# A decoder layer on one core: the scaling of the key rows moved to GpSimd, the second value copy of each row to ScalarE

## Chip, cores and metric

One core of a Trainium2 chip runs the whole kernel in one launch. The metric is the device time of one execution in microseconds, the median of several runs. Engines: TensorE (PE; PEld are its weight loads), VectorE (DVE), ScalarE (ACT), GpSimd (POOL), SyncE (SP), which issues the DMAs. Each engine works through its own program in order and waits for the others by semaphores.

## What is computed

```python
x = layernorm(x + attn(x))            # x: (2, 256, 512); 32 heads of 16, ALiBi, causal
x = layernorm(x + cross(x, ctx))      # ctx: (2, 512, 512); 32 query heads, 8 key/value heads of 128
x = layernorm(x + ffn(x))             # 16 groups of 32 -> 128 -> 32, gelu

# cross attention, the part that the change touches:
kv = concatenate([ctx, x], axis=1)    # 768 rows for each of the 2 samples, 1536 in all
k = (kv @ Wk).reshape(..., 8, 128)
v = (kv @ Wv).reshape(..., 8, 128)
k = k * rsqrt(mean(k * k, -1) + 1e-6) * k_norm_w
```

Products are kept exact to float32 by splitting each operand into a high and a low part and making three passes (hi x hi, hi x lo, lo x hi).

## The kernel before

There are three stages: self-attention with the keys and values of cross-attention (function `self_attention_and_keys`), cross-attention, feed-forward. The change lies in the first.

**Self-attention** goes by 16 quads of four heads. For quad c, TensorE makes the scores S(c) (L699). Then for each of four heads i: VectorE adds the ALiBi bias and takes the row's extreme (E, `softmax_shift`, L514); ScalarE takes the exponential and its sum (E, L398); VectorE takes reciprocals of two heads' sums at a time (R, L523); GpSimd multiplies by them (R, `normalise`, L349 and L351) and makes the bias for the next quad (`alibi`, L344); TensorE transposes (T(c,i), L709); VectorE copies the result out of PSUM (L529). Each second quad TensorE weighs the values (PV, L721), and ScalarE (A, L405) and VectorE (A, L535) split the result into high and low.

**Key and value rows** are 12 rows n of 128 tokens, eight of ctx and four of x after the first layernorm. The work of a row on TensorE is cut into eight parts (n,0) to (n,7), two for each group of 512 columns: parts 0 and 1 make the first half of the keys (g = 0), 2 and 3 the second (g = 1), 4 and 5 the first half of the values, 6 and 7 the second. A part is six 128x512 matmuls. `g_ps` counts finished groups. What follows a group:
- keys, g: ScalarE copies PSUM to `k_rows` (L422, at part 2 or 4) and squares it (L427); VectorE sums (L554) and makes the mean plus epsilon (`k_ms`, L557, at part 3 or 5); GpSimd raises to -1/2 (`k_inv`, L377, same part); VectorE multiplies `k_rows` in place by `k_inv`, broadcast over 128 columns (L564, at part 5 for g = 0 and 7 for g = 1); TensorE transposes in the next row's parts 1 and 3 (KT(n,g), L738); ScalarE copies to `kT_st` with the norm weights (L412).
- values: VectorE copies PSUM to `v_st` (`take_values`, L543), the first half at part (n,6), the second at part (n+1,0).
- SyncE stores `v_st` when `vg_out` has counted both halves (L307), and `kT_st` when `kt_out` has (L309), and before the next stage's first load waits for all stores.

x rows come late: Y and LN (L606 to L612), the power for the layernorm on GpSimd (L380), X1 (L620), transposes XT (L794), and their split by ScalarE (L483) and VectorE (L615).

**Order.** `order_of_work` (L81 to L150) writes out one list for all engines; each engine runs the entries that concern it, in that order. Row parts stand between the steps of the quads, so that TensorE has matmuls while the other engines do the softmax. An excerpt, from quad 13 on: `S14, (8,0), E(14,0), T(13,0), KT(7,0), (8,1), E(14,1), T(13,1), (8,2), E(14,2), T(13,2), KT(7,1), (8,3), E(14,3), R(14,0), T(13,3), R(14,1), S15, PV6, (8,4), E(15,0), A6, T(14,0), (8,5), E(15,1), T(14,1)`. Around row 6: `E(10,2), T(9,2), (6,0), XT1, E(10,3), R(10,0), T(9,3), KT(5,0)`. Around quad 4: `(2,3), W7, R(4,1), S5, PV1`, where W7 is four 128x512 subtractions on GpSimd (L336).

**PSUM.** Transposes and PV share banks 4 and 7 in turn (RING), the row groups share 5 and 6 (GROUPS). Before it writes a bank TensorE waits until the last user has been drained (`drained`, L633 to L653): after a T for VectorE's copy, after a PV for VectorE's low half, after a KT for ScalarE, after a second x1 transpose for VectorE's low half, after a value group for `vg_out`.

Of the kernel before, what the change touches and what calls it, by code (L numbers as in the profile page):

```python
# [12 lines left out]
P = 128  # L13
ALU = mybir.AluOpType
ACT = mybir.ActivationFunctionType
# [137 lines left out]
def self_attention_and_keys(nc, d, k):  # L153

    with ExitStack() as ctx:
# [68 lines left out]
        kinv_made, knrm_made = t.sem("kinv_made"), t.sem("knrm_made")  # L224
        vg_out = t.sem("vg_out")
        kt_ps, kt_out = t.sem("kt_ps"), t.sem("kt_out")
# [41 lines left out]
        def _(sp):  # L268
# [31 lines left out]
            for n in range(ROWS):  # L300
                if n + 2 < B * CT:
                    load_context(n + 2)
                if n == 1:
                    load_weights(7)
                if n == 4:
                    load_weights(8)
                sp.wait_ge(vg_out, 2 * n + 2)  # L307
                sp.dma_start(v_view[:, :, rows_of(n), :], v_st[:]).then_inc(v_store, 16)
                sp.wait_ge(kt_out, 2 * n + 2)  # L309
                sp.dma_start(k_view[:, :, rows_of(n), :], kT_st[:]).then_inc(k_store, 16)  # L310
# [6 lines left out]
        def _(pool):  # L317
# [44 lines left out]
            for what, a in ORDER:  # L362
# [8 lines left out]
                elif what == "part":  # L371
                    n, r = a
                    if r in (3, 5) and n < ROWS:
                        g = r // 2 - 1
                        w = slice(GH * g, GH * (g + 1))
                        pool.wait_ge(kms_made, 2 * n + g + 1)
                        nc.gpsimd.tensor_tensor(k_inv[:, w], k_ms[:, w], minus_half[:, w], ALU.pow).then_inc(kinv_made, 1)  # L377
                elif what == "LN":
                    pool.wait_ge(var_made, a + 1)
                    nc.gpsimd.tensor_tensor(rstd[:, a:a + 1], var[:, a:a + 1], minus_half[:, 0:1], ALU.pow)\  # L380
                        .then_inc(rstd_made, 1)

        @block.scalar
        def _(act):
# [29 lines left out]

            def part(n, r):
                if r in (2, 4) and n < ROWS:
                    g = r // 2 - 1
# [73 lines left out]
        def _(dve):  # L491
# [46 lines left out]

            def take_values(n, g):
                dve.wait_ge(g_ps, 4 * n + g + 3)  # L540
                if n >= 1:
                    dve.wait_ge(v_store, 16 * n)
                nc.vector.tensor_copy(v_st[:, GH * g:GH * (g + 1), :].rearrange("p h e -> p (h e)"),  # L543
                                      bank[:, bank_of("part", (n, 4 + 2 * g)), :]).then_inc(vg_out, 1)

            def part(n, r):
                if r == 0 and n >= 1:
                    take_values(n - 1, 1)
                if n == ROWS:
# [8 lines left out]
                if r == 6:  # L558
                    take_values(n, 0)
                if r in (5, 7):  # L560
                    g = r // 2 - 2
                    w = slice(GH * g, GH * (g + 1))
                    dve.wait_ge(kinv_made, 2 * n + g + 1)
                    nc.vector.tensor_tensor(k_rows[:, w, :], k_rows[:, w, :], k_inv[:, w].rearrange("p (h a) -> p h a", a=1)  # L564
                                            .to_broadcast([P, GH, HD]), ALU.mult).then_inc(knrm_made, 1)

# [65 lines left out]
        def _(pe):  # L632
            def drained(what, a):  # L633
# [12 lines left out]
                elif held == "XT":  # L646
                    pe.wait_ge(x1t_lo, i + 1)
                elif held == "Y":
                    pe.wait_ge(y_sum, i + 1)
                elif i[1] < 4:  # L650
                    pe.wait_ge(kg_out, 2 * i[0] + i[1] // 2 + 1)
                else:
                    pe.wait_ge(vg_out, 2 * i[0] + i[1] // 2 - 1)  # L653

# [1056 lines left out]
```

## Time and profile before

| | us |
|---|---|
| median of 3 runs | 885.67 (884.92 to 885.82) |
| profiled execution | 883.53 |
| its span | 881.7 |
| TensorE busy | 834.4 (95%) |
| VectorE busy | 567.6 (64%) |
| GpSimd busy | 505.6 (57%) |
| ScalarE busy | 462.6 (52%) |

The first stage takes about the first 283 us of the span. In rows of groups the columns are: line, engine, operation, output<-input, shapes, count; then busy time in us and mean ns of one; then the engine's idle time before them and who ended it. In rows of the timeline: start and duration in us, engine, line, operation, and in brackets the engine's idle time before it and who ended that. Consecutive instructions of one engine overlap by some 0.1 us.

### The profile page before, as it was taken

What the parts mean: (1) busy time and instruction counts of PE and PEld (TensorE: products, weight loads), DVE (VectorE), ACT (ScalarE), POOL (GpSimd) and SP (SyncE); (2) the same over time, 40 slices, a digit from 0 to 9 for tenths busy, and PEclk for the clock granted to TensorE, in tenths of its full rate; (3) what the DMA queues carried; (4) which work ended last, traced back from release to release, by engine and by line L of the source; (5) the groups of instructions that cost most, each with busy time, mean ns of one, the idle gap of its engine ahead of it and who ended that gap; (6) DMA issues with size and microseconds to landing.
All of it is one profiled execution on the core that took longest, in us unless ns stands there. A gap on an engine that the chain in (4) does not pass through costs nothing. (4 is left out here: it accounts for less than half of the span.)

```text
span 881.7 us, 15131 instructions
## 1 busy us (share of the span) xinstructions
PE 834.4 (95%) x4833; PEld 698.2 (79%) x4833; DVE 567.6 (64%) x1538; ACT 462.6 (52%) x981; POOL 505.6 (57%) x655
## 2 busy tenths in 40 slices
PE   7999999899898699999999999999999999999975
PEld 5777776677676688888888888888888888888753
DVE  4377675777542576676677667667667767777535
ACT  5666653555322365555556456555555645556242
POOL 2565863665311786756765775775675676445711
PEclk9999999999999699999999999999999999999978
DMA  6503132121113621121121122122121102000011
GB/s 223 183 26 132 63 100 81 56 64 49 48 48 96 222 67 66 36 67 67 37 65 65 36 65 65 36 65 65 36 65 65 36 12 67 1 1 1 0 25 48
DMA packets 48463, 56.23 MB, mean 64 GB/s; under 512 B 4622, under 2 KB 29724, under 8 KB 48412
## 3 DMA queue, kind: packets, MB, share of 16 engines
q1 hardware_dynamic: 48412, 55.59, 20.0%
q8 instruction: 27, 0.44, 0.2%
q14 instruction: 24, 0.20, 0.1%
HBM read 41.95 MB, written 13.63 MB: 63 GB/s over the span
## 5 line engine op out<-in xcount | busy, mean ns | idle before, releaser
L1090 POOL TENSOR_SCALAR prob<-prob,x_rinv 128x768 f32<-128x768 f32 x128 | 116.2, 908 | 166.8 <-DVE x_rinv L1265 166.8
L1207 ACT ACTIVATE pT_hi<-bank 128x512 fp32r<-128x512 f32 x192 | 114.4, 597 | 96.6 <-PE bank L1422 96.0
L1186 ACT ACTIVATE prob<-bank,x_nm,q_rms 128x768 f32<-128x768 f32 x128 | 127.1, 993 | 49.2 <-DVE x_nm L1259 48.9
L1256 DVE TENSOR_REDUCE x_mx<-bank 128x1 f32<-128x768 f32 x128 | 122.1, 954 | 26.3 <-PE bank L1380 26.2
L1318 DVE TENSOR_TENSOR pT_lo<-bank,pT_hi 128x512 fp32r<-128x512 f32 x192 | 130.4, 680 | 8.5 <-ACT pT_hi L1207 6.9
L1422 PE MATMUL bank<-ident,prob 128*128 128x128 f32 x768 | 116.2, 274 | 5.3 <-POOL prob L1090 5.3
L1422 PEld LDWEIGHTS bank<-ident,prob 128*128 128x128 f32 x768 | 95.8, 141 | 17.6 <-POOL prob L1090 6.4
L398 ACT ACTIVATE s_self<-s_self,nm_self 128x128 f32<-128x128 f32 (+1 forms) x128 | 57.0, 447 | 66.5 <-DVE nm_self L514 66.4
L48 PE MATMUL bank<-pT_hi,xv_hi 128*128 128x512 f32 x192 | 86.6, 451 | 0.9 <-DVE pT_lo L1318 0.8
L50 PE MATMUL bank<-pT_hi,xv_lo 128*128 128x512 f32 x192 | 75.8, 395 | 0.0
L49 PE MATMUL bank<-pT_lo,xv_hi 128*128 128x512 f32 x192 | 75.4, 393 | 0.0
L1380 PE MATMUL bank<-xk_hi,qT_hi 128*128 128x384 f32 x256 | 69.3, 352 | 2.5 <-DVE xk_lo L1284 2.4
L1380 PE MATMUL bank<-xk_lo,qT_hi 128*128 128x384 f32 x256 | 67.2, 344 | 0.0
L1380 PE MATMUL bank<-xk_hi,qT_lo 128*128 128x384 f32 x256 | 67.1, 343 | 0.0
L48 PE MATMUL bank<-w_hi,cT_hi 128*128 128x512 f32 x128 | 56.3, 440 | 1.2 <-DVE x_rows L606 1.2
L377 POOL TENSOR_TENSOR k_inv<-k_ms,minus_half 128x4 f32<-128x4 f32 x24 | 27.7, 1155 | 50.3 <-DVE k_ms L557 49.8
L1216 ACT ACTIVATE oT_hi<-bank 128x512 fp32r<-128x512 f32 x32 | 19.1, 598 | 70.3 <-PE bank L50 70.3
L1380 PEld LDWEIGHTS bank<-xk_hi,qT_hi 128*128 128x128 f32 x256 | 46.7, 193 | 11.3 <-issue 2.8
L48 PE MATMUL bank<-wo_hi,oT_hi 128*128 128x512 f32 x128 | 52.2, 408 | 0.0
L48 PE MATMUL bank<-wq_hi,x_hi 128*128 128x512 f32 x128 | 51.9, 406 | 0.0
L49 PE MATMUL bank<-w_lo,cT_hi 128*128 128x512 f32 x128 | 50.6, 395 | 0.0
L50 PE MATMUL bank<-w_hi,cT_lo 128*128 128x512 f32 x128 | 50.5, 395 | 0.0
(196 smaller groups left out, 2042.8 us busy)
## 6 DMA issues: line engine op xcount, KB each, us to landing
wo_raw<-in_Wo SPq DMA_DIRECT2D x8, 1024.0 KB, 5.4
wq_raw<-in_Wq SPq DMA_DIRECT2D x7, 1024.0 KB, 5.5
v_by_head<-v_st SPq DMA_DIRECT2D x12, 512.0 KB, 3.3
kT_by_head<-kT_st SPq DMA_DIRECT2D x12, 512.0 KB, 3.2
xk_raw<-kT_by_head SPq DMA_DIRECT2D x16, 384.0 KB, 3.2
xv_raw<-v_by_head SPq DMA_DIRECT2D x16, 384.0 KB, 3.1
wq_raw<-in_w_attn SPq DMA_DIRECT2D x12, 256.0 KB, 4.4
xk_raw<-in_ctx SPq DMA_DIRECT2D x8, 256.0 KB, 2.5
```

Source lines behind the costliest of these rows:

```text
L48: nc.tensor.matmul(out, a_hi, b_hi, start=first, stop=False)
L49: nc.tensor.matmul(out, a_hi, b_lo, start=False, stop=False)
L50: return nc.tensor.matmul(out, a_lo, b_hi, start=False, stop=last)
L377: nc.gpsimd.tensor_tensor(k_inv[:, w], k_ms[:, w], minus_half[:, w], ALU.pow).then_inc(kinv_made, 1)
L398: nc.scalar.activation(s_sb[:, c % 2, i, a:e], s_sb[:, c % 2, i, a:e], ACT.Exp, bias=nm[:, c % 2, i, qt:qt + 1], scale=-1.0, accum_out=rsu ...
L1090: nc.gpsimd.tensor_scalar(prob[:, s, :], prob[:, s, :], rinv[:, s:s + 1], 1.0, ALU.mult, ALU.mult)\
L1186: nc.scalar.activation(prob[:, s, :].rearrange("p (a e) -> p a e", a=2), bank[:, at:at + 2, 0:HALF], ACT.Exp, bias=nm[:, s:s + 1], scale=q ...
L1207: nc.scalar.activation(pT_hi[:, a, :], bank[:, turn.bank[s, what, a], :], ACT.Copy)\
L1256: nc.vector.reduce_max(mx[:, s:s + 1], bank[:, at:at + 2, 0:HALF], AX.XY)\
L1318: nc.vector.tensor_tensor(pT_lo[:, a, :], bank[:, turn.bank[s, what, a], :], f32(pT_hi[:, a, :]), ALU.subtract).then_inc(ring_out, 1)
L1380: last = nc.tensor.matmul(bank[:, at + c, 0:HALF], a_hi[:, g, w], k_part[:, b, c * HALF:(c + 1) * HALF], start=start, stop=stop)
L1422: last = nc.tensor.transpose(bank[:, at, j * P:(j + 1) * P], prob[:, UT * (s % 2) + j, a * P:(a + 1) * P], ident[:])
```

## The change

The product of `k_rows` and `k_inv` is issued by GpSimd, right behind the power of the same g at parts 3 and 5 and behind a wait for that power, where VectorE issued it at parts 5 and 7. The copy of the second value half, at part (n+1,0), is issued by ScalarE, at the head of that part, and counts on a semaphore of its own, `vg_late`; the first half stays on VectorE. SyncE and TensorE wait for the two semaphores accordingly.

```diff
--- before.py
+++ after.py
@@ -222,7 +222,7 @@
         g_ps = t.sem("group_ps")
         kg_out, ksq_made, kss_made, kms_made = t.sem("kg_out"), t.sem("ksq_made"), t.sem("kss_made"), t.sem("kms_made")
         kinv_made, knrm_made = t.sem("kinv_made"), t.sem("knrm_made")
-        vg_out = t.sem("vg_out")
+        vg_out, vg_late = t.sem("vg_out"), t.sem("vg_late")
         kt_ps, kt_out = t.sem("kt_ps"), t.sem("kt_out")
         q_ps, q_rows_out, ss_part = t.sem("q_ps_cross"), t.sem("q_rows_out"), t.sem("ss_part1")
         k_store, v_store = t.sem("k_store"), t.sem("v_store")
@@ -304,7 +304,8 @@
                     load_weights(7)
                 if n == 4:
                     load_weights(8)
-                sp.wait_ge(vg_out, 2 * n + 2)
+                sp.wait_ge(vg_out, n + 1)
+                sp.wait_ge(vg_late, n + 1)
                 sp.dma_start(v_view[:, :, rows_of(n), :], v_st[:]).then_inc(v_store, 16)
                 sp.wait_ge(kt_out, 2 * n + 2)
                 sp.dma_start(k_view[:, :, rows_of(n), :], kT_st[:]).then_inc(k_store, 16)
@@ -375,6 +376,9 @@
                         w = slice(GH * g, GH * (g + 1))
                         pool.wait_ge(kms_made, 2 * n + g + 1)
                         nc.gpsimd.tensor_tensor(k_inv[:, w], k_ms[:, w], minus_half[:, w], ALU.pow).then_inc(kinv_made, 1)
+                        pool.wait_ge(kinv_made, 2 * n + g + 1)
+                        nc.gpsimd.tensor_tensor(k_rows[:, w, :], k_rows[:, w, :], k_inv[:, w].rearrange("p (h a) -> p h a", a=1)
+                                                .to_broadcast([P, GH, HD]), ALU.mult).then_inc(knrm_made, 1)
                 elif what == "LN":
                     pool.wait_ge(var_made, a + 1)
                     nc.gpsimd.tensor_tensor(rstd[:, a:a + 1], var[:, a:a + 1], minus_half[:, 0:1], ALU.pow)\
@@ -413,6 +417,12 @@
                                      bank[:, bank_of("KT", (n, g)), :], ACT.Copy, scale=nw[:]).then_inc(kt_out, 1)
 
             def part(n, r):
+                if r == 0 and n >= 1:
+                    act.wait_ge(g_ps, 4 * n)
+                    if n >= 2:
+                        act.wait_ge(v_store, 16 * (n - 1))
+                    nc.scalar.activation(v_st[:, GH:KVH, :].rearrange("p h e -> p (h e)"),
+                                         bank[:, bank_of("part", (n - 1, 6)), :], ACT.Copy).then_inc(vg_late, 1)
                 if r in (2, 4) and n < ROWS:
                     g = r // 2 - 1
                     w = slice(GH * g, GH * (g + 1))
@@ -536,16 +546,14 @@
                                                scalar=cols[:, 2 * KT + m:2 * KT + m + 1], in1=f32(xT_hi[:, m, w]),
                                                op0=ALU.add, op1=ALU.subtract).then_inc(at_lo, 1)
 
-            def take_values(n, g):
-                dve.wait_ge(g_ps, 4 * n + g + 3)
+            def take_values(n):
+                dve.wait_ge(g_ps, 4 * n + 3)
                 if n >= 1:
                     dve.wait_ge(v_store, 16 * n)
-                nc.vector.tensor_copy(v_st[:, GH * g:GH * (g + 1), :].rearrange("p h e -> p (h e)"),
-                                      bank[:, bank_of("part", (n, 4 + 2 * g)), :]).then_inc(vg_out, 1)
+                nc.vector.tensor_copy(v_st[:, 0:GH, :].rearrange("p h e -> p (h e)"),
+                                      bank[:, bank_of("part", (n, 4)), :]).then_inc(vg_out, 1)
 
             def part(n, r):
-                if r == 0 and n >= 1:
-                    take_values(n - 1, 1)
                 if n == ROWS:
                     return
                 if r in (3, 5):
@@ -556,13 +564,7 @@
                     dve.wait_ge(kss_made, 2 * n + g + 1)
                     nc.vector.tensor_scalar(k_ms[:, w], k_ss[:, w], 1.0 / HD, RMS_EPS, ALU.mult, ALU.add).then_inc(kms_made, 1)
                 if r == 6:
-                    take_values(n, 0)
-                if r in (5, 7):
-                    g = r // 2 - 2
-                    w = slice(GH * g, GH * (g + 1))
-                    dve.wait_ge(kinv_made, 2 * n + g + 1)
-                    nc.vector.tensor_tensor(k_rows[:, w, :], k_rows[:, w, :], k_inv[:, w].rearrange("p (h a) -> p h a", a=1)
-                                            .to_broadcast([P, GH, HD]), ALU.mult).then_inc(knrm_made, 1)
+                    take_values(n)
 
             for j in range(TT):
                 dve.wait_ge(xt_hi, j + 1)
@@ -649,8 +651,10 @@
                     pe.wait_ge(y_sum, i + 1)
                 elif i[1] < 4:
                     pe.wait_ge(kg_out, 2 * i[0] + i[1] // 2 + 1)
+                elif i[1] == 4:
+                    pe.wait_ge(vg_out, i[0] + 1)
                 else:
-                    pe.wait_ge(vg_out, 2 * i[0] + i[1] // 2 - 1)
+                    pe.wait_ge(vg_late, i[0] + 1)
 
             pe.wait_ge(const, 4)
             for j in range(TT):
```

## Rows read from the trace of the kernel before

**Rows 1.** Windows view, the changed stage: stretch, then busy us of each engine.
```profile
45.00:283.00 238.00, 225.44 (x1508) 174.07 (x1506) 149.16 (x508) 118.95 (x356) 117.39 (x222) 1.00 0.22 68
```

**Rows 2.** Table of waits in the stage: waiter, releaser, total us, times, longest.
```profile
PE bank L709 <- DVE pT_self L529: 3.3, 3, 2.0
```

**Rows 3.** Groups in the stage: busy us, mean ns, idle before and releaser.
```profile
L564 DVE TENSOR_TENSOR k_rows<-k_rows,k_inv 128x512 f32<-128x512 f32 x24 | 16.9, 706 | 0.9 <-POOL k_inv L377 0.9
...
L377 POOL TENSOR_TENSOR k_inv<-k_ms,minus_half 128x4 f32<-128x4 f32 x24 | 27.7, 1155 | 50.3 <-DVE k_ms L557 49.8
...
L543 DVE COPY v_st<-bank 128x512 f32<-128x512 f32 x24 | 16.3, 679 | 1.3 <-PE bank L50 1.2
...
L422 ACT ACTIVATE k_rows<-bank 128x512 f32<-128x512 f32 x24 | 14.0, 582 | 3.0 <-PE bank L50 3.0
...
L361 POOL TENSOR_TENSOR x_rows<-x_rows,pT_self 128x512 f32<-128x512 f32 x4 | 5.1, 1304 | 0.0
```

**Rows 4.** Timeline, VectorE and GpSimd side by side: start, us, engine, line.
```profile
77.91 0.17 DVE L557 TENSOR_SCALAR k_ms<-k_ss 128x4 f32<-128x4 f32 x1
...
77.99 0.69 DVE L564 TENSOR_TENSOR k_rows<-k_rows,k_inv 128x512 f32<-128x512 f32 x1
...
78.16 1.38 POOL L377 TENSOR_TENSOR k_inv<-k_ms,minus_half 128x4 f32<-128x4 f32 x1 [3.01 <-DVE k_ms L557]
...
96.16 0.86 DVE L557 TENSOR_SCALAR k_ms<-k_ss 128x4 f32<-128x4 f32 x1
```

**Rows 5.** Timeline around KT(0,0).
```profile
64.53 0.69 DVE L564 TENSOR_TENSOR k_rows<-k_rows,k_inv 128x512 f32<-128x512 f32 x1 [0.38 <-POOL k_inv L377]
...
66.39 0.63 PE L738 MATMUL bank<-ident,k_rows 128*128 128x128 f32 x4 [0.71 <-DVE pT_self L529]
```

**Rows 6.** Timeline at S(14).
```profile
201.30 0.94 PE L699 MATMUL bank<-kT_even,qT 32*128 32x128 f32 x16 [0.61 <-DVE nm_self L514]
```

**Rows 7.** Timeline, T(15,0) and T(15,1), and the value copy between.
```profile
222.10 0.55 PE L709 MATMUL bank<-ident,s_self 128*128 128x128 f32 x3 [1.09 <-POOL s_self L351]
...
225.21 0.68 DVE L543 COPY v_st<-bank 128x512 f32<-128x512 f32 x1
...
226.50 0.52 PE L709 MATMUL bank<-ident,s_self 128*128 128x128 f32 x3 [2.02 <-DVE pT_self L529]
```

**Rows 8.** Timeline before T(9,2).
```profile
157.68 0.89 DVE L564 TENSOR_TENSOR k_rows<-k_rows,k_inv 128x512 f32<-128x512 f32 x1
...
162.59 0.52 PE L709 MATMUL bank<-ident,s_self 128*128 128x128 f32 x3 [0.92 <-DVE pT_self L529]
```

**Rows 9.** Timeline, GpSimd's normalisation of quad 4 and T(4,2).
```profile
96.98 0.88 POOL L349 TENSOR_SCALAR s_self<-s_self,rinv_self 128x128 f32<-128x128 f32 x1
...
97.84 0.47 POOL L351 TENSOR_SCALAR s_self<-s_self,rinv_self 128x256 f32<-128x256 f32 x1
...
98.83 0.49 PE L709 MATMUL bank<-ident,s_self 128*128 128x128 f32 x3
```

**Rows 10.** Timeline, second x1 transpose's ScalarE half and KT(5,0).
```profile
165.80 0.58 ACT L483 ACTIVATE x_hi<-bank 128x512 fp32r<-128x512 f32 x1
...
167.24 0.63 PE L738 MATMUL bank<-ident,k_rows 128*128 128x128 f32 x4 [1.30 <-DVE x_lo L615]
```

**Rows 11.** Timeline from the power of row 8 to T(14,1).
```profile
209.52 1.01 POOL L377 TENSOR_TENSOR k_inv<-k_ms,minus_half 128x4 f32<-128x4 f32 x1 [3.11 <-DVE k_ms L557]
...
212.78 0.29 DVE L514 CUSTOM_DVE_ANT_0 s_self<-bank,alibi 128x128 f32<-128x128 f32 x1 [1.46 <-POOL alibi L344]
...
214.90 0.48 DVE L535 SCALAR_TENSOR_TENSOR x_lo<-bank,cols,x_hi 128x256 fp32r<-128x256 f32 x1 [1.48 <-ACT x_hi L405]
...
215.67 0.49 PE L709 MATMUL bank<-ident,s_self 128*128 128x128 f32 x3
```

**Rows 12.** Timeline, normalisation of quad 1 and T(1,0).
```profile
58.04 0.48 POOL L351 TENSOR_SCALAR s_self<-s_self,rinv_self 128x256 f32<-128x256 f32 x1
...
59.99 0.49 PE L709 MATMUL bank<-ident,s_self 128*128 128x128 f32 x3
```

## Prediction

> **What bounds the kernel.** I read five views, in this order. First the page: TensorE is busy for most of the span, so only its idle time can shrink. Then the windows view of the changed stage, from the first key row's work to the last key transposes [rows 1]: TensorE is busy 225.44 of 238.00 us, so 12.6 us is all that any relief of another engine can give. VectorE is busy 149.16, ScalarE 118.95 and GpSimd 117.39 us there: none is full, and what counts is when each answers. The table of waits [rows 2] says who was late: mostly VectorE. The groups give prices [rows 3]; the timeline gives each stall its place. TensorE has 14 stalls there; below are the ones that the change can touch. The rest have nothing removed or added just ahead of them, and I leave them.
>
> **What is removed.** VectorE loses 24 products of 706 ns and 12 value copies of 679 ns [rows 3]: 16.9 + 8.1 = 25.1 us. That is no gain by itself; it counts where TensorE stands waiting for VectorE with a removed instruction shortly before.
> - KT(0,0), 0.71 us [rows 5]: it waits for a bank that VectorE drains, and VectorE had first waited 0.38 us for the inverse norm and then scaled for 0.69. Both go: all 0.7 is regained.
> - S(14), 0.61 us [rows 6]: it waits for the last shift of quad 13. Ahead of that stand, in VectorE's order, both products of row 7, some 0.6 us each with the overlap. Gain 0.6, all that TensorE waits.
> - T(15,1), 2.02 us [rows 7]: it waits for the copy of T(15,0), which VectorE makes after a value copy that started at 225.21. That copy leaves: some 0.6, less 0.1 for what comes late upstream (below), so 0.5. The four weight subtractions before it remain.
> - T(9,2), 0.92 us [rows 8]: a product of 0.89 us at 157.68 is in the chain, but the next shift also needs a bias from GpSimd, which will be later. Between 0 and 0.9; I take 0.3, near the low end, as the bias follows closely.
>
> Sum of gains: 0.7 + 0.6 + 0.5 + 0.3 = 2.1 us.
>
> **What GpSimd pays.** 24 products at 128x512. The trace has no broadcast operand on GpSimd; the nearest row is the in-place addition of the same size, 1304 ns [rows 3]. The low end is VectorE's own 706 ns; the high end is 1.30 plus one VectorE product waited out, 0.69: 2.0 us. I take 1.30, the same engine, size and kind. The handoff from the power to the product through GpSimd's own semaphore is not shown; across engines it took 0.08 us (78.08 to 78.16 [rows 4]), and I take that: 1.38 us per product, 33 us in all, behind each of the 24 powers (1155 ns). Some comes back: a power took 1.38 us while VectorE's product ran beside it, against 1.01 alone [rows 4, 11], and 0.88 us went into a 128x128 normalisation beside one [rows 9]. That is 0.4 to 0.5 us for each collision, and these products leave.
>
> The rows put the product at 1304 ns on GpSimd against 706 on VectorE [rows 3]. The Trainium skill speaks against such a move (GPSIMD Engine Reference, Elementwise — side-by-side cycle accounting): a two-input operation costs GpSimd about twice VectorE's time, 4497 ns at 2048 elements. By proportion, an estimate from that page is 1.12 us for 512, by which the sum below would be 0.2 us better, the cost at T(4,2) halved.
>
> Queued behind the product are normalisations and biases, and behind these TensorE's transposes and VectorE's shifts. Site by site:
> - T(1,0): its normalisation ended at 58.52 and TensorE came at 59.99 [rows 12]: slack 1.47 against 1.38. No cost, narrowly. T(9,0) stands the same way.
> - T(4,2): normalisation over at 98.31, TensorE at 98.83 [rows 9]: slack 0.52. The shift is 1.38 less the 0.5 of the collision that leaves, 0.88. Cost 0.35.
> - T(14,1): a power at 209.52 stands before the normalisation and the bias that VectorE waited 1.46 us for; then come shift, exponential, ScalarE's and VectorE's halves of the attention output, whose end (215.38) frees the bank that T(14,1) takes at 215.67 [rows 11]. 1.38 - 0.29 = 1.1 us late. But T(15,0) stalls 1.09 us for another reason [rows 7], VectorE having two products in between; without them VectorE has caught up to within 0.1. So this cost is swallowed by that stall: nothing, apart from the 0.1 above, and T(15,0) gives nothing.
> - Elsewhere GpSimd was idle before its next work for longer than 1.4 us, or the collision returned the difference. There the product costs nothing; if that cover went, each would cost up to 1.4.
> - The reverse collision: k_ms took 0.86 us beside a GpSimd subtraction [rows 4]. The product starts after k_ms and a power, when VectorE mostly reads PSUM; nothing, at most 0.7 once or twice.
>
> **What ScalarE pays.** 12 copies at 582 ns [rows 3], 7.0 us. It waits for the group that VectorE waited for, at the same place in its order, and queued behind are exponentials, key evictions and the x1 halves. In most rows ScalarE is waiting for the next shift then: nothing, and 0.6 each if it weren't. One place is bare: in row 6 the copy stands between an exponential and the second x1 half, which already ran back to back at 165.80, and TensorE waited 1.30 us for its other half [rows 10]. Cost 0.6.
>
> **Queues.** The value store gets two waits for one and is issued when the later copy is done, 0.1 us sooner. The end of the stage is set by the last key store, behind the last key transposes, for which the last product comes a whole group of TensorE work early. No DMA is added, and GpSimd's queue has none. The two later stages are untouched.
>
> **Sum.** -2.1 + 0.35 + 0.6 = -1.15 us. The profiled execution took 883.53 us (span 881.7 and 1.8 around it), so I expect 882.4 with a span of 880.5. The median of the runs is 885.67, 2.1 above the profiled one; carried over: 884.5 us. What a measurement of this kernel can tell from no change is about 0.2%, 1.8 us.
>
> **Rivals.**
> (a) GpSimd becomes the late engine. The place is the normalisation behind a power; it decides from a product of 1.39 us, where the 1.47 of T(1,0) is used up with the handoff. At 2.0 us (2.08 with handoff): T(1,0) and T(9,0) 0.6 each, T(4,2) 1.1, T(14,1) 1.8 of which 1.1 is swallowed, 0.7, and ScalarE's 0.6: 3.6 us. The gains at KT(0,0), T(9,2) and T(15,1) go, since each needs GpSimd's next bias or normalisation early; 0.6 is left at S(14): +3.0, so 888.7. For it: slacks that equal the price to 0.1 us; against: all additions and subtractions of this size lie near 1.3. Chance 0.18, all sizes of it.
> (b) All of VectorE's stalls close: 0.71 + 0.92 + 0.61 + 2.02 and GpSimd's 1.09 at T(15,0) [rows 5 to 8] are 5.35 us, so 880.3 at the most; half of it, 883.0, is the likelier form. For it: VectorE is the releaser of nearly all. Against: behind several stands ScalarE's half or a weight subtraction, which stay. Chance 0.17.
> (c) Nothing moves: what VectorE gives up was hidden, and later joints between the engines re-form each stall. 885.7. For it: VectorE is only 63% busy in the stage (149.16 of 238). Chance 0.15.
> The forecast, small gains against smaller losses, has 0.50.
>
> **How the numbers follow.** The forecast case spreads by about 1 us either way, as it is a difference of five small terms: a fifth of it lies beyond 1.8 us faster, hardly any beyond 1.8 slower. With most of (b), faster by over 0.2% gets 0.25; with most of (a), slower gets 0.16; the rest, 0.59, is within. The range takes in half of (b), all of (c) and (a) up to a product of about 1.7 us: 882.4 to 887.6.
>
> **What would show it.** Right: the GpSimd product at 1.2 to 1.4 us; powers uniformly near 1.02; the stalls at KT(0,0) and S(14) gone, that of T(15,1) near 1.5, T(15,0)'s below 0.3; new stalls at T(4,2) (0.3) and T(14,1) (1.0); the one at KT(5,0) grown to 1.9. TensorE's idle time in the stage near 11.4. Wrong: a product above 1.45 us with new GpSimd stalls at T(1,0) and T(9,0), or fewer than 10 us idle, or a changed start of the next stage's transposes apart from the shift.

## The result, and the profile after

The kernel after takes **879.52 us** (median of 7 runs, 879.4 to 881.52) against 884.92 (7 runs of the kernel before beside it, 882.54 to 886.67): ratio 0.9948, 95% interval 0.9932 to 0.9963. That is 4.6 us faster by the ratio, four times the forecast of 1.15, and outside the range of 882.4 to 887.6 on the fast side. Its span is 877.6 us against 881.7.

The windows view of the changed stage, as in [rows 1], once over the same stretch and once cut where the stage now ends: TensorE's first transposes of the next stage (L1369, after L1373) moved from 287.63 to 284.24, 3.39 us, and 283.00 - 3.39 = 279.61.

```profile
45.00:283.00 238.00, 225.10 (x1509) 174.13 (x1507) 128.43 (x472) 126.25 (x368) 136.57 (x246) 1.00 0.23 71
...
45.00:279.61 234.61, 225.10 (x1509) 174.13 (x1507) 128.43 (x472) 125.71 (x368) 136.57 (x246) 1.00 0.22 69
```

TensorE's idle time in the stage is 234.61 - 225.10 = 9.5 us, where it was 12.6 and the forecast had 11.4. VectorE lost 20.7 us there, GpSimd gained 19.2, ScalarE 6.8.

Who TensorE waited for (table of waits, 45 to 283: waiter, releaser, total, times, longest), to be held against [rows 2] and [rows 5 to 10]:

```profile
PE bank L742 <- DVE x_lo L617: 1.8, 1, 1.8
PE bank L713 <- POOL s_self L350: 1.4, 1, 1.4
...
PE bank L713 <- DVE pT_self L539: 0.9, 2, 0.5
PE bank L713 <- DVE x_lo L545: 0.8, 1, 0.8
...
PE bank L713 <- POOL s_self L352: 0.2, 1, 0.2
```

The largest is KT(5,0), grown as foreseen; the 1.4 is T(15,1), shrunk; the 0.9 are T(9,2) and T(9,3); 0.8 is the new T(14,1), 0.2 the new T(4,2). KT(0,0), S(14), T(15,0) and a stall that the prediction had not listed, KT(4,0), are gone. The groups of after in the same stretch, the counterparts of [rows 3]:

```profile
L352 POOL TENSOR_SCALAR s_self<-s_self,rinv_self 128x256 f32<-128x256 f32 x64 | 31.5, 493 | 0.0
L350 POOL TENSOR_SCALAR s_self<-s_self,rinv_self 128x128 f32<-128x128 f32 x64 | 25.1, 392 | 19.5 <-DVE rinv_self L533 18.8
L380 POOL TENSOR_TENSOR k_rows<-k_rows,k_inv 128x512 f32<-128x512 f32 x24 | 25.0, 1040 | 1.9
L378 POOL TENSOR_TENSOR k_inv<-k_ms,minus_half 128x4 f32<-128x4 f32 x24 | 24.6, 1023 | 43.2 <-DVE k_ms L565 42.8
...
L553 DVE COPY v_st<-bank 128x512 f32<-128x512 f32 x12 | 8.2, 681 | 0.6 <-PE bank L50 0.6
L424 ACT ACTIVATE v_st<-bank 128x512 f32<-128x512 f32 x12 | 7.0, 583 | 6.6 <-PE bank L50 6.5
```

The product on GpSimd takes **1040 ns**, not 1304; the power fell from 1155 to 1023 (23 of the 24 lie at 1.01 to 1.03 us, one at 1.24). The timeline of after at the places of the steps: quad 1's normalisation behind a power and its product and T(1,0) [rows 12], KT(0,0) without a wait, T(4,2), the ScalarE copy ahead of the second x1 half, KT(5,0), T(14,1), T(15,1):

```profile
56.71 1.03 POOL L378 TENSOR_TENSOR k_inv<-k_ms,minus_half 128x4 f32<-128x4 f32 x1 [2.09 <-DVE k_ms L565]
57.82 1.04 POOL L380 TENSOR_TENSOR k_rows<-k_rows,k_inv 128x512 f32<-128x512 f32 x1
58.84 0.37 POOL L350 TENSOR_SCALAR s_self<-s_self,rinv_self 128x128 f32<-128x128 f32 x1
59.20 0.48 POOL L352 TENSOR_SCALAR s_self<-s_self,rinv_self 128x256 f32<-128x256 f32 x1
...
60.03 0.49 PE L713 MATMUL bank<-ident,s_self 128*128 128x128 f32 x3
...
65.58 0.60 PE L742 MATMUL bank<-ident,k_rows 128*128 128x128 f32 x4
...
97.98 0.55 PE L713 MATMUL bank<-ident,s_self 128*128 128x128 f32 x3 [0.23 <-POOL s_self L352]
...
163.25 0.57 ACT L424 ACTIVATE v_st<-bank 128x512 f32<-128x512 f32 x1
163.72 0.58 ACT L493 ACTIVATE x_hi<-bank 128x512 fp32r<-128x512 f32 x1
...
165.18 0.63 PE L742 MATMUL bank<-ident,k_rows 128*128 128x128 f32 x4 [1.78 <-DVE x_lo L617]
...
213.90 0.52 PE L713 MATMUL bank<-ident,s_self 128*128 128x128 f32 x3 [0.82 <-DVE x_lo L545]
...
223.12 0.52 PE L713 MATMUL bank<-ident,s_self 128*128 128x128 f32 x3 [1.41 <-POOL s_self L350]
```

At T(1,0) the handoff from power to product through GpSimd's own semaphore cost 57.82 - 57.74 = 0.08 us, as assumed. The normalisation ends at 59.68 instead of 58.52, 1.16 later, and TensorE comes at 60.03: slack 0.35, no stall.

**The measure used below.** "The stage" is the time from TensorE's first stall of the stretch, at S(2) near 58 us (0.52 us in every kernel), to its first transposes of the next stage. It leaves out the start and the later stages. All other figures are TensorE's stalls in us, a dash is none. Each row is read from the timeline of one profiled execution. Below, TensorE's "lead" at a place is how much earlier it starts the same matmul than in the kernel compared with.

```
                       stage   KT(0,0) CT3 T(4,2) KT(4,0) T(9,2) KT(5,0) S(14) T(14,1) T(15,0) T(15,1)
before                 230.41   0.71   0.45  -     0.88    0.92   1.30   0.61    -      1.09    2.02
after                  226.97    -     0.21 0.23    -      0.48   1.78    -     0.82     -      1.41
after again (a1)       228.26*   -     0.22 0.22    -      0.48   1.78    -     0.82     -      1.42
before again (c0)      233.67** 0.71  0.49  -     0.89    0.93   1.30   0.61    -      1.10    2.02
product alone (e1)     227.12    -     0.31 0.16    -      0.49   1.30    -     0.84     -      2.02
copy alone (e2)        230.15   0.71   0.22  -     0.88    0.92   1.78   0.62    -      1.11    1.43
no product (e3)        225.19    -     0.22  -      -      0.31   1.78    -      -       -      1.42
product twice (e4)     236.25**  -     0.84 0.71   1.14    0.59   1.78    -     1.93     -      0.73
(4,0) put back (e5)    229.16*   -     0.22 0.25   0.44    0.49   1.78    -     0.84     -      1.42
copy behind XT1 (e6)   226.43    -     0.21 0.23    -      0.49   1.29    -     0.82     -      1.41
and two later (e7)     224.88    -     0.21  -      -      0.48   1.29    -      -       -      1.42
W8 spread too (e8)     224.92*   -     0.22  -      -      0.48   1.30    -      -       -       -
only (4,1) moved (e9)  230.14   0.72   0.47  -     0.44    0.93   1.30   0.62    -      1.15    2.01
```

CT3 is the transposition of the fourth row of ctx. Each star marks a dip of TensorE's granted clock in the stage; by the leads ahead of it and behind it each costs 1.3 to 1.6 us (last section). The other stalls of the stage are the same within 0.02 us in all of them but two: e4 has the further ones named with it, and e2 one of 0.30 us at scores near 102 us.

### The profile page after: what moved, and what is told of

Read it like the earlier page. It is cut to its first block and busy times, and to the rows that moved or that the text cites. A ratio compares the mean times of both kernels' runs of the same rounds, so it can differ in the third digit from the quotient of the medians.

```text
span 877.6 us, 15143 instructions
## 1 busy us (share of the span) xinstructions
PE 834.1 (95%) x4833; PEld 696.8 (79%) x4833; DVE 546.5 (62%) x1502; ACT 469.4 (53%) x993; POOL 524.5 (60%) x679
## 5 line engine op out<-in xcount | busy, mean ns | idle before, releaser
L1220 ACT ACTIVATE oT_hi<-bank 128x512 fp32r<-128x512 f32 x32 | 19.2, 599 | 70.3 <-PE bank L50 70.3
L539 DVE COPY pT_self<-bank 128x384 f32<-128x384 f32 x64 | 35.4, 552 | 27.8 <-PE bank L713 27.7
```

The lines of the kernel that those rows point to most:

```text
L539: nc.vector.tensor_copy(pT[:, c % 2, i, :], bank[:, bank_of("T", (c, i)), 0:3 * P]).then_inc(pt_out, 1)
```

## The experiments

**One half of the change at a time.** e1 moves the product alone, e2 the copy alone. The edit of e1 to the kernel after:

```diff
             def part(n, r):
-                if r == 0 and n >= 1:
-                    act.wait_ge(g_ps, 4 * n)
...
+                if r == 0 and n >= 1:
+                    take_values(n - 1, 1)
```

and of e2 (the same kernel with the products of the kernel before):

```diff
                         nc.gpsimd.tensor_tensor(k_inv[:, w], k_ms[:, w], minus_half[:, w], ALU.pow).then_inc(kinv_made, 1)
-                        pool.wait_ge(kinv_made, 2 * n + g + 1)
-                        nc.gpsimd.tensor_tensor(k_rows[:, w, :], k_rows[:, w, :], k_inv[:, w].rearrange("p (h a) -> p h a", a=1)
-                                                .to_broadcast([P, GH, HD]), ALU.mult).then_inc(knrm_made, 1)
```

> Only the product moves to GpSimd; both value copies stay on VectorE. Theory A (the gain comes from the product, because it stood in stretches where VectorE works without a pause up to the reciprocals): TensorE's stalls at KT(0,0), KT(4,0) and S(14) are gone, T(9,2) near 0.5, KT(5,0) back at 1.30, T(15,1) near 2.0; the next stage's first transposes start 2.7 to 3.3 us earlier than before, ratio 0.9955 to 0.997. Theory B (either edit frees VectorE enough, half the gain each): 1.5 to 2 us earlier, and KT(4,0)'s stall is only shortened.

> Only the second value copy moves, to ScalarE; the products stay on VectorE. Theory A: KT(0,0) shorter by the copy that stood before it (0.71 to 0.1 or less), T(15,1) 2.02 to 1.4, KT(5,0) 1.30 to 1.8, KT(4,0) stays at 0.88 and S(14) at 0.61; the next stage's first transposes 0.5 to 1.0 us earlier than before. Theory B: 1.5 to 2 us earlier.

Measured: e1 880.11 us (879.19 to 882.19, 6 runs), ratio to before 0.9946 [0.9924, 0.9967], stage 3.29 us shorter than before. e2 884.17 us (880.74 to 885.32, 12 runs), ratio 0.9986 [0.9970, 1.0002], stage 0.26 shorter. Together 3.55 against 3.44 for both at once: the two add up, and **the product is nearly the whole of it**. e2 came out under its expected 0.5 to 1.0 us, and KT(0,0) stayed at 0.71 where 0.1 was expected: the product alone closes it. The copy has two main terms, and beside them 0.23 gained at CT3 and 0.30 lost at the scores near 102 us. The wait at T(15,1) with the copy moved (e2), timeline:

```profile
226.06 0.52 PE L716 MATMUL bank<-ident,s_self 128*128 128x128 f32 x3 [1.43 <-POOL s_self L350]
```

and the same place and KT(5,0) with the copy left on VectorE (e1):

```profile
165.75 0.63 PE L735 MATMUL bank<-ident,k_rows 128*128 128x128 f32 x4 [1.30 <-DVE x_lo L612]
...
224.32 0.52 PE L706 MATMUL bank<-ident,s_self 128*128 128x128 f32 x3 [2.02 <-POOL s_self L351]
```

T(15,1) goes from 2.02 to 1.43 by the copy alone, KT(5,0) from 1.30 to 1.78 by the copy alone.

**What the product costs on GpSimd's path.** e3 leaves the product out on both engines.

```diff
-                        pool.wait_ge(kinv_made, 2 * n + g + 1)
-                        nc.gpsimd.tensor_tensor(k_rows[:, w, :], k_rows[:, w, :], k_inv[:, w].rearrange("p (h a) -> p h a", a=1)
-                                                .to_broadcast([P, GH, HD]), ALU.mult).then_inc(knrm_made, 1)
...
-                pe.wait_ge(knrm_made, 2 * n + g + 1)
+                pe.wait_ge(kinv_made, 2 * n + g + 1)
```

> The changed kernel with the product left out on every engine: the key rows aren't divided by their norm. It shows what the 24 products cost on GpSimd. If their price on the path is what the stalls at T(4,2) (0.23) and T(14,1) (0.82) and the late biases say, this is 0.5 to 1.5 us faster than the changed kernel, with both stalls gone. If GpSimd's products are wholly hidden: within 0.3 us of it.

Measured: 879.32 us (876.62 to 879.93, 6 runs), ratio 0.9932 [0.9910, 0.9954]; stage 225.19. So 24 products of 1.04 us, 25 us of GpSimd's time, cost 226.97 - 225.19 = 1.78 us on the path, a little over the expected 0.5 to 1.5. The table says where: T(4,2) 0.23, T(14,1) 0.82, T(9,2) 0.17 as stalls. TensorE's lead of e3 over the kernel after grows at the same three places, by 0.4, 1.0 and 0.2 us. The whole time doesn't show it: the medians are 879.32 and, for the kernel after, 879.52 and 880.2, and the intervals overlap.

**Rival (a), GpSimd as the late engine.** e4 puts a second product in place behind each one, by ones.

```diff
+                                                .to_broadcast([P, GH, HD]), ALU.mult).then_inc(ktwice_made, 1)
+                        pool.wait_ge(ktwice_made, 2 * n + g + 1)
+                        nc.gpsimd.tensor_tensor(k_rows[:, w, :], k_rows[:, w, :], k_one[:, w].rearrange("p (h a) -> p h a", a=1)
                                                 .to_broadcast([P, GH, HD]), ALU.mult).then_inc(knrm_made, 1)
```

> The changed kernel with each product followed by a second one of the same form by ones, so that GpSimd pays 1.04 us and a handoff 24 times more. By the prediction's rival of a late GpSimd, whose slack at T(1,0) and T(9,0) is now 0.35 and 0.22 us: new stalls there of 0.8 and 0.9, T(4,2) 1.2, T(14,1) 1.8; together 3 to 5 us slower than the changed kernel, so no faster than the kernel before. If GpSimd has room beyond that: less than 1.5 us slower.

Measured: 889.48 us (886.66 to 891.78, 12 runs), ratio to before **1.0042** [1.0023, 1.0060]: slower than before. The stage is 236.25 us, 9.3 longer than after. By the leads its two clock dips make up 3.1 of that, so some 6.2 belong to the second product, where 3 to 5 were expected. Without the dips it would still be longer than before's 230.41. The groups of e4:

```profile
L387 POOL TENSOR_TENSOR k_rows<-k_rows,k_one 128x512 f32<-128x512 f32 x24 | 25.0, 1043 | 1.9
L384 POOL TENSOR_TENSOR k_rows<-k_rows,k_inv 128x512 f32<-128x512 f32 x24 | 25.0, 1040 | 1.9
```

and its timeline at the place that the rival named, T(1,0):

```profile
59.87 1.04 POOL L387 TENSOR_TENSOR k_rows<-k_rows,k_one 128x512 f32<-128x512 f32 x1
60.89 0.38 POOL L354 TENSOR_SCALAR s_self<-s_self,rinv_self 128x128 f32<-128x128 f32 x1
...
61.77 0.55 PE L721 MATMUL bank<-ident,s_self 128*128 128x128 f32 x3 [0.65 <-POOL s_self L356]
```

TensorE stalls 0.65 us at T(1,0), 0.68 at T(9,0), 0.71 at T(4,2), 1.93 at T(14,1), and, unexpected, 0.94 at KT(0,1) and 1.14 at KT(4,0). The mechanism of the rival is real, and another 1.1 us per product turns the gain into a loss. With 1.04 us the product stays under the 1.39 at which the slack of T(1,0) is used up; but T(1,0) and T(9,0) are only part of e4's loss, and no run shows at which price between 1.04 and 2.1 us the gain ends.

**KT(4,0), the stall that the prediction left aside.** The timeline of the kernel before ahead of it, VectorE and GpSimd side by side:

```profile
129.94 0.68 DVE L554 TENSOR_REDUCE k_ss<-k_sq 128x4 f32<-128x512 f32 x1
130.65 0.17 DVE L557 TENSOR_SCALAR k_ms<-k_ss 128x4 f32<-128x4 f32 x1
130.73 0.68 DVE L564 TENSOR_TENSOR k_rows<-k_rows,k_inv 128x512 f32<-128x512 f32 x1
...
134.10 0.17 DVE L523 RECIPROCAL rinv_self<-rsum_self 128x4 f32<-128x4 f32 x1
...
134.38 0.37 POOL L349 TENSOR_SCALAR s_self<-s_self,rinv_self 128x128 f32<-128x128 f32 x1 [2.10 <-DVE rinv_self L523]
134.63 0.68 DVE L564 TENSOR_TENSOR k_rows<-k_rows,k_inv 128x512 f32<-128x512 f32 x1
134.73 0.93 POOL L351 TENSOR_SCALAR s_self<-s_self,rinv_self 128x256 f32<-128x256 f32 x1
...
137.09 0.29 DVE L514 CUSTOM_DVE_ANT_0 s_self<-bank,alibi 128x128 f32<-128x128 f32 x1 [1.02 <-POOL alibi L344]
...
139.84 0.63 PE L738 MATMUL bank<-ident,k_rows 128*128 128x128 f32 x4 [0.88 <-DVE x_lo L535]
```

From 129.94 to the reciprocals at 134.10 VectorE works without a gap, with the product (4,0) in that stretch. GpSimd has waited 2.10 us for them. Its second instruction then takes 0.93 instead of 0.48 us beside the product (4,1). Behind it come the bias that VectorE waits 1.02 us for (so that VectorE's own 0.68 for the product (4,1) isn't what is late), a shift, an exponential, both halves of A and at last the bank for KT(4,0). So two products work on this stall from 9 and 5 us ahead, neither of them just before it. e5 puts only the product (4,0) back on VectorE; e9 is the kernel before with only (4,1) moved.

```diff
+                if (n, r) == (4, 5):
+                    w = slice(0, GH)
+                    dve.wait_ge(kinv_made, 2 * n + 1)
+                    nc.vector.tensor_tensor(k_rows[:, w, :], k_rows[:, w, :], k_inv[:, w].rearrange("p (h a) -> p h a", a=1)
+                                            .to_broadcast([P, GH, HD]), ALU.mult).then_inc(knrm_back, 1)
```

```diff
+                        if (n, g) == (4, 1):
+                            pool.wait_ge(kinv_made, 2 * n + g + 1)
+                            nc.gpsimd.tensor_tensor(k_rows[:, w, :], k_rows[:, w, :], k_inv[:, w].rearrange("p (h a) -> p h a", a=1)
+                                                    .to_broadcast([P, GH, HD]), ALU.mult).then_inc(knrm_moved, 1)
...
-                if r in (5, 7):
+                if r in (5, 7) and (n, r) != (4, 7):
```

> The changed kernel with one product of 24, row 4's first, back on VectorE at its old place. Theory A (VectorE works without a pause from this product through two shifts, a copy and a value copy to the reciprocals of quad 8, behind which GpSimd's bias, the shift, ScalarE's and VectorE's halves and KT(4,0) follow): KT(4,0)'s stall, 0.88 before and none after, comes back at 0.6 to 0.9, all others stay within 0.2 of the changed kernel's. Rival: the stall went because GpSimd was quicker without collisions, or because the copy left: then it stays away.

> The kernel before with one product of 24, row 4's second, on GpSimd. Row 4's first, put back on VectorE in the changed kernel, brought back 0.44 of KT(4,0)'s 0.88 us. Theory: the other half was a collision, a 128x256 normalisation of quad 8 that took 0.93 us instead of 0.48 beside row 4's second product, and the bias behind it came later by that. Then KT(4,0)'s stall is 0.4 to 0.5 here, that normalisation takes 0.48, and no other stall moves by over 0.1. Rival: both halves are VectorE's own lateness; then the stall stays at 0.8 or more.

Measured in e5 (one run, 881.57 us) and e9 (one run, 884.68 us, beside 887.56 for before). Timeline of e5:

```profile
133.57 0.37 POOL L351 TENSOR_SCALAR s_self<-s_self,rinv_self 128x128 f32<-128x128 f32 x1 [0.98 <-DVE rinv_self L536]
133.93 0.48 POOL L353 TENSOR_SCALAR s_self<-s_self,rinv_self 128x256 f32<-128x256 f32 x1
...
138.60 0.63 PE L753 MATMUL bank<-ident,k_rows 128*128 128x128 f32 x4 [0.44 <-DVE x_lo L548]
```

Timeline of e9:

```profile
135.90 0.37 POOL L350 TENSOR_SCALAR s_self<-s_self,rinv_self 128x128 f32<-128x128 f32 x1 [0.98 <-DVE rinv_self L528]
136.25 0.48 POOL L352 TENSOR_SCALAR s_self<-s_self,rinv_self 128x256 f32<-128x256 f32 x1
...
140.93 0.63 PE L746 MATMUL bank<-ident,k_rows 128*128 128x128 f32 x4 [0.44 <-DVE x_lo L540]
```

Both have the product (4,0) on VectorE and (4,1) on GpSimd, and both stall 0.44: moving (4,1) takes away the collision (0.93 to 0.48) and with it 0.88 - 0.44 = 0.44 us; moving (4,0) takes the other 0.44, and TensorE, which in e5 was 0.60 us behind the kernel after once past this point, gains that. e5 brought back less than the 0.6 to 0.9 expected; e9, which tests where the rest went, came out as expected. The stall is settled, in both its halves.

**Taking the two costs away.** e6 moves the ScalarE copy of row 5 behind the second x1 half; e7 does that and issues the products (2,0) and (8,0), those ahead of T(4,2) and T(14,1), at part 5 instead of behind their powers.

```diff
             def part(n, r):
-                if r == 0 and n >= 1:
+                if r == 0 and n >= 1 and n != 6:
+                    late_values(n)
...
+                    if a == 1:
+                        late_values(6)
```

```diff
+            LATER = ((2, 0), (8, 0))
...
+                    if (n, r - 5) in LATER:
+                        scale_keys(n, r - 5)
...
+                        if (n, g) not in LATER:
+                            scale_keys(n, g)
```

> The changed kernel with row 5's second value copy, which stands between an exponential and the second x1 half in ScalarE's order, put behind that half. If this copy is what lengthened KT(5,0)'s stall (1.30 to 1.78 us): the stall is back at 1.2 to 1.35 and the next stage starts 0.5 us earlier than in the changed kernel. If it was lateness from elsewhere: no change.

> As the one before, and on GpSimd two of the 24 products, row 2's first and row 8's first, put two parts later, behind the normalisations and biases that now queue behind them. If those products cause the new stalls at T(4,2) (0.23 us) and T(14,1) (0.82 us), both are gone, and the next stage starts 1.2 to 1.6 us earlier than in the changed kernel, unless T(15,0)'s stall of 1.09 us, which hid the second, comes back with up to 0.8. Time: 0.5 to 1.8 us under the changed kernel.

Measured: e6 879.53 us (878.37 to 881.48, 6 runs), ratio 0.9934 [0.9912, 0.9955]; KT(5,0) back at 1.29, stage 0.54 shorter than after. That shows the 0.48 to be the copy's place in ScalarE's order; the copy on ScalarE is free there once it stands behind the x1 half. The whole time is the same as after's (879.52 and 880.2): half a microsecond can't be told there. e7 879.07 us (877.66 to 881.04, 6 runs), ratio 0.9925 [0.9903, 0.9947]; stage 224.88, 2.09 shorter than after (1.2 to 1.6 expected) and 1.55 than e6. T(4,2) and T(14,1) no longer stall:

```profile
212.03 1.04 POOL L352 TENSOR_TENSOR k_rows<-k_rows,k_inv 128x512 f32<-128x512 f32 x1
212.13 0.49 PE L727 MATMUL bank<-ident,s_self 128*128 128x128 f32 x3
213.19 1.01 POOL L388 TENSOR_TENSOR k_inv<-k_ms,minus_half 128x4 f32<-128x4 f32 x1
```

The product (8,0) now runs at 212.03, behind the bias that it had delayed, and T(14,1) at 212.13 has no wait. The stall at T(15,0) did not come back either, so of the two terms that swallow each other in the kernel after, here the one is avoided and the other kept as gain.

**The rest of T(15,1).** Its 1.4 us stand behind four VectorE subtractions of W8, which e8 (e7 with this edit) spreads, one behind each copy of quad 15. The kernel after and e7 were repeated beside it.

```diff
-                if what == "W" and a in ON_VECTOR:
+                if what == "W" and a in ON_VECTOR and a != 8:
...
                     take_transposed(*a)
+                    if a[0] == NQ - 1:
+                        early_lo(8, a[1])
```

> The changed kernel once more, on the same chip as the next two. The stalls of the first stage repeat within 0.1 us. If the spread between executions (one of the two profiles of the kernel before was 4 us longer than the other) comes from a granted clock that falls for some microseconds at places of their own, then windows of 6 us show it in any profile that is longer, and none in one that isn't.

> The kernel with the two later products and the late copy again, beside the changed kernel. Its first stage was 2.1 us shorter by the profile; so its median is 1.5 to 2.5 us under the changed kernel's. If something later gives that back, under 0.5 us.

> As the one before, and VectorE makes the four late weight subtractions (two inputs in SBUF) one behind each copy of quad 15, where it made all four before them. T(15,1)'s stall of 1.42 us waits for the copy behind these subtractions or for a normalisation that took 1.32 us beside them instead of 0.37: it should fall under 0.3, those normalisations to 0.4 to 0.9, and the next stage start 1.0 to 1.5 us earlier. If the first cross-attention product then waits for the last subtraction, the gain is given back there.

Measured, all against the same runs of before: after 880.2 us (878.81 to 881.63), ratio 0.9938 [0.9919, 0.9957]; e7 again 876.73 (875.71 to 881.2), 0.9917 [0.9891, 0.9943]; e8 877.75 (874.16 to 879.68), 0.9907 [0.9882, 0.9931]; 6 runs each. e7's median is 3.5 us under after's, more than the 1.5 to 2.5 expected, and more than its stage explains. The stall at T(15,1) is gone in e8 (timeline; the first two rows are for the last section):

```profile
220.89 0.68 DVE L527 TENSOR_TENSOR first_wq_lo<-wq_raw,first_wq_hi 128x512 fp32r<-128x512 f32 x1
220.90 1.02 POOL L360 TENSOR_SCALAR s_self<-s_self,rinv_self 128x256 f32<-128x256 f32 x1
...
222.04 0.49 PE L729 MATMUL bank<-ident,s_self 128*128 128x128 f32 x3
```

Its stage is nevertheless no shorter than e7's in the profile, 224.92, because that execution had a clock dip of about 1.4 us. Nor does e8 part the two things that T(15,1) could wait for: in the kernel after a normalisation took 1.32 us and the next 1.42 beside the four subtractions, and the copy of T(15,0) stood behind them; spreading them brought both forward. These are the two lowest medians of all, 8.4 and 7.4 us under before's 885.16. Their intervals overlap that of after and each other's: that e7 beats after is shown in the stage (2.09 us, the same in two profiles: 224.88 and 224.87), while the whole time agrees (876.73 beside 880.2) without proving it. **Whether e8 adds to e7 stays open.**

**The kernel before a second time**, no edit, to see how far one execution's profile can be trusted:

> The kernel before, profiled a second time. It shows what differs between two profiles of one program. In the first profile the next stage took 15.6 us from its first transposes to its first attention transposes, in the changed kernel 15.2. If the change did that, it is 15.6 again here; if it is how transfers happen to land, anything from 14.9 to 15.7. The first stage's stalls repeat to 0.1 us by either.

Measured: one run, 887.48 us, span 885.7, 4.0 more than the first profile, with the stalls of the table the same to 0.04 us. The difference lies in the granted clock (last section): 3.3 of the 4.0 are in the stage.

## Why the prediction was wrong, point by point

The direction and the mechanism of every term that was listed held; what failed is the list, and with it the size. The stage's idle time, 9.5 us, fell under the 10 that the prediction had named as a sign of being wrong. In the order of its steps, gain or loss of TensorE as the experiments gave it:

- **"The rest have nothing removed or added just ahead of them, and I leave them"**: the step that failed. KT(4,0) gave 0.88 as a stall, about 1.05 in TensorE's lead over the kernel before, and CT3 (below) is of the same kind. TensorE's lead at the next stage is 3.39 us where the forecast had 1.15; of the 2.24 between them KT(4,0) is nearly half, and no other term is over 0.3. The list of stalls was screened by looking for a removed instruction just ahead of the releaser; what finds this one is to follow the releaser's own chain back to the last place where an engine worked without a gap. There it meets VectorE's unbroken 129.94 to 134.27, with a product in it, and a GpSimd instruction stretched by another.
- **GpSimd product at 1.30 us**: 1.04. The row taken, an addition of two full operands, was the nearest and still another form: a multiplication with a broadcast second operand takes 1.04. Whether the operand or the operation makes the difference no run separates. The estimate from the page of the Trainium skill (GPSIMD Engine Reference, Elementwise — side-by-side cycle accounting), 1.12 for 512 elements, was nearer, 8% above what was measured for the product (and 14% under the 1304 ns of the addition in [rows 3]). The handoff was 0.08 as assumed. Effect: everything behind a power is 1.16 us late, not 1.38, T(4,2) stalls 0.23 (0.38 in the lead) for 0.35, T(14,1) 0.82 for 1.1.
- **KT(0,0) 0.7**: the stall's 0.71 closed, by the product alone (e1 none, e2 0.71), and TensorE's lead after it is 0.84 to 0.97.
- **S(14) 0.6**: 0.61 closed and nothing new there. Right.
- **T(9,2) 0.3**, chosen near the low end of 0 to 0.9: 0.44. With no product at all it is 0.61 (e3), so the bias that comes later took 0.17, not 0.6.
- **T(15,1) 0.5**: 0.61. The copy gives 0.59 of it alone (e2).
- **KT(5,0) cost 0.6**: 0.48. Right in place and cause, shown by e6.
- **T(14,1), swallowed by T(15,0)**: right. TensorE's lead was 2.74 us before T(14,1), 1.77 after it and 2.78 behind T(15,0): 1.0 lost and given back.
- **CT3**: 0.45 to 0.21, not foreseen at all; the copy alone does it (e2 0.22), the product alone does half (e1 0.31).

Sum by leads: 0.96 at KT(0,0) with what follows, with CT3 and the rest to 1.23 at T(4,1); -0.38 at T(4,2) leaves 0.85; about 1.05 at KT(4,0) makes 1.97 at T(8,1) (0.92 stood at T(8,0)); 0.14 at T(9,1), without a stall of its own, and 0.45 at T(9,2) make 2.55; -0.48 at KT(5,0) makes 2.07; 0.68 at S(14) makes 2.75; T(14,1) and T(15,0) cancel; 0.60 at T(15,1) makes 3.38. The next stage starts 3.39 earlier.

**Rival (b)**, half of VectorE's stalls closing, 883.0, was nearer in kind: of its 5.35 us 0.71 + 0.44 + 0.61 + 0.61 + 1.09 = 3.46 closed as stalls, where the T(15,0) part was paid for by T(14,1). It too missed KT(4,0), which was in no list. **Rival (a)** decides between 1.04 and 2.1 us of product, as e1 and e4 bracket it, and its own figure, 1.39, lies between. The **reverse collision**, put at nothing, is small but there: in the kernel after `k_ms` took 0.25 to 0.45 us instead of 0.17 at four places; no run ties a stall of TensorE's to it.

**What stays open** is the rest of the 4.1 us in the span: 3.4 are in the stage, 0.4 more between the next stage's first transposes and its first attention transposes (15.60 us before, 15.17 after), 0.3 later. Over the other profiles that stretch runs from 14.63 (e6) to 15.62 (e3), 15.23 in the second profile of before: it varies that much without the change, and no run ties it to the change. Open too is why the medians differ by more than the profiles, 4.6 us by the ratio against 4.1. One thing on record bears on it. Of the 46 runs of before beside the experiments, 19 have a mean granted clock of 0.977 or 0.979, and they took 885.8 to 888.42 us; the 27 others took 881.69 to 887.14. None of the 13 runs of after is under 0.980. So the kernel before goes through its long executions more often; that the closed stalls are the reason is not shown.

## What to carry to other kernels

List every stall of the engine that sets the time, and follow each one back through its releasers until an engine is found that had been working without a gap; an instruction taken out of that unbroken stretch counts, even 9 us and several joints ahead of the stall. When work goes to a slower engine, the question isn't its sum of busy time (25 us here, of which 1.8 reached the path) but the slack of what is queued behind each single piece, and the few pieces without slack can be issued later, as e7 did. Measure the moved instruction in its own form of operands before trusting a row of another form.

## What was not expected of the hardware

**Collisions between GpSimd and VectorE** are sized by [rows 4, 9] and the runs. The kernel before has powers of 1.38 us and normalisations of 0.88 and 0.93 beside VectorE's products; with those gone the mean power went from 1155 to 1023 ns (groups above). It is the products that do it: the mean is 1025 ns in e1 and 1155 in e2. Left over are the pairs with the weight subtractions, whose operands are both in SBUF too. The timeline of e8, above, has one at 220.90: 0.54 us more for an instruction of 0.48, and no loss to VectorE's 0.68: GpSimd is the one that pays here. It isn't always: the `k_ms` of 0.86 us beside a GpSimd subtraction [rows 4] is there in the kernel after too, at 95.00 with 0.90.

**The granted clock dips inside this busy stage** in some executions and not in others of the same program. Windows of the kernel before in its second profile (columns as in [rows 1]; the clock is the third number from the end):

```profile
162.00:168.00 6.00, 3.78 (x22) 2.54 (x20) 4.95 (x15) 2.93 (x10) 1.28 (x2) 1.00 0.01 3
168.00:174.00 6.00, 5.59 (x58) 3.90 (x58) 2.17 (x12) 3.20 (x10) 4.66 (x12) 0.72 0.27 87
```

and the same windows of the first profile of before:

```profile
162.00:168.00 6.00, 3.72 (x22) 2.80 (x23) 4.95 (x16) 3.19 (x11) 0.35 (x2) 1.00 0.17 56
168.00:174.00 6.00, 6.00 (x68) 4.28 (x67) 1.94 (x8) 3.89 (x13) 4.69 (x12) 1.00 0.10 31
```

TensorE stalls 0.93, 0.40 and 1.30 us within 5 us here, at T(9,2), T(9,3) and KT(5,0), and was busy 3.78 of 6 us ahead of the dip and 3.72 of 6 where none came. The mean of 0.72 lies between the two levels of 2.4 and 1.2 GHz, so the window held both. A second dip, 228 to 234, also 0.72, follows the stalls of T(15,0) and T(15,1). The second profile of after, e5 and e8 dip between 162 and 174 (0.80 to 0.92). e4 dips at the same place (168 to 180: 0.88 and 0.84) and again from 222 to 228 (0.72), where its stall of 1.93 us at T(14,1) lies. The nine other profiles stay at 1.00 from 162 to 234. Closing stalls in such a cluster could also make the dips rarer; the runs are too few to say.
